# First value sums ahead of the scaled rows, products between flips and their users, and a second tensor in the row scaling: the first part of a two-layer gated cross-attention kernel

## The reference

```python
x = x + tanh(g_xattn[0]) * L0_xattn(layernorm(x), ctx)     # this part
x = x + tanh(g_ffn[0])   * L0_ffn(layernorm(x))            # shared GEGLU (this part), 8 experts by argmax
x = x + tanh(g_xattn[1]) * L1_xattn(ctx, ctx, layernorm(x))
x = x + tanh(g_ffn[1])   * L1_ffn(layernorm(x))
```

```python
Q = (x @ Wq.T).reshape(16, 16).T        # [i, h]
K, V = likewise from ctx                # [j, h]
A = softmax(einsum('ih,jh->ij', Q, K) / 4)
out = einsum('ij,jh->ih', A, V).T.reshape(256) @ Wo.T
```

## Time and profile before

| | |
|---|---|
| median of 3 runs | 764.0 us (761.69 to 764.12) |
| the profiled execution's own time | 763.81 us |
| its span in the trace | 762.0 us |
| busy in the span | PE 91%, PEld 78%, DVE 83%, POOL 55%, ACT 51% |
| the first part | 0 to about 316 us |
| mean granted TensorE clock | 0.98 |

### The profile page before, as it was taken

The page is one execution under the profiler, slowest core; times in us unless marked ns, Lnnn a source line. Parts: engine busy times, 40 slices in busy tenths (PEclk is TensorE's granted clock), DMA queues, the critical chain, the costliest instruction groups (busy, mean ns, idle before and its releaser), DMA issues.

```text
span 762.0 us, 12814 instructions
## 1 busy us (share of the span) xinstructions
PE 693.1 (91%) x4381; PEld 591.8 (78%) x4381; DVE 633.2 (83%) x927; ACT 392.3 (51%) x699; POOL 422.1 (55%) x304
## 2 busy tenths in 40 slices
PE   6749999999999989889999999999976999999996
PEld 4428878787878778657788888888865999989986
DVE  3889999999999964789999999999887777678653
ACT  2313443344343421247777777777743565555643
POOL 3788888888888881413998666667032111110000
PEclk9958999999999999989999999999999999999999
DMA  9501010011118012140544426100010101000000
GB/s 274 215 15 42 29 28 28 28 28 34 49 40 348 8 62 70 31 172 16 199 157 180 182 91 249 29 28 22 15 35 28 39 19 56 29 28 8 16 15 21
DMA packets 28642, 56.43 MB, mean 74 GB/s; under 512 B 3408, under 2 KB 24656, under 8 KB 27440
## 3 DMA queue, kind: packets, MB, share of 16 engines
q1 hardware_dynamic: 23408, 47.64, 17.6%
q0 software_dynamic: 1872, 5.11, 2.4%
q10 hardware_dynamic: 3312, 3.02, 1.2%
HBM read 48.55 MB, written 7.21 MB: 73 GB/s over the span
## 4 chain that ended last, share of the span: by engine, by line
PE 49%; DVE 19%; POOL 12%; issue 10%; ACT 7%; DMA 2%; DVEq 0%; SPq 0%; POOLq 0%; ACTq 0%
PE bank L747 19%; PE bank L738 16%; PE bank L999 9%; POOL PRODV L624 8%; PE bank L755 4%; DVE PRODQ L1562 2%; POOL PRODV L626 2%; DVE SLOT_r L1950 2%; DVE bank L1571 2%; DVE PRODV_r L1950 2%; DVE bank L1652 2%; DVE STC L2038 1%; ACT L1468 1%; ACT XS L1468 1%; ACT L1288 1%
## 5 line engine op out<-in xcount | busy, mean ns | idle before, releaser
L624 POOL TENSOR_TENSOR PRODV<-SHARED 128x2048 f32<-128x2048 f32 x32 | 144.7, 4522 | 30.4 <-DVE bank L1652 25.0
L738 PE MATMUL bank<-ROWS,SLOT 128*128 128x128 f32 x1024 | 122.9, 279 | 0.0
L738 PEld LDWEIGHTS bank<-ROWS,SLOT 128*128 128x128 f32 x1024 | 120.5, 195 | 0.8
L717 POOL TENSOR_TENSOR RS<-VE,MHALF 128x2 f32<-128x2 f32 x16 | 13.1, 819 | 149.3 <-DVE VE L2045 149.3
L626 POOL TENSOR_TENSOR PRODV<-PRODV 128x1024 f32<-128x1024 f32 x32 | 74.7, 2336 | 2.5
L1571 DVE TENSOR_REDUCE bank<-PRODQ 128x256 f32<-128x4096 f32 x16 | 70.7, 4419 | 0.1
L1562 DVE TENSOR_TENSOR PRODQ<-bank,SHARED 128x4096 f32<-128x4096 f32 x16 | 70.6, 4413 | 0.0
L1950 DVE TENSOR_TENSOR PRODQ_r<-SLOT,ROWS_r 128x1024 fp32r<-128x1024 f32 x44 | 63.5, 1472 | 0.8 <-ACT ROWS_r L1375 0.6
L641 POOL DMA_INDIRECT XS<-normal_rows,INV x23 | 26.8, 1164 | 64.5 <-PE bank L755 42.8
L738 PE MATMUL bank<-SLOT,HA 128*128 128x256 f32 x256 | 58.3, 381 | 2.4 <-DVE HA L1760 2.4
L1950 DVE TENSOR_TENSOR W_r<-SLOT,PRODQ_r 128x1024 fp32r<-128x1024 f32 x44 | 58.6, 1332 | 1.7 <-ACT PRODQ_r L1342 1.7
(11 more groups left out here) (275 smaller groups left out, 1912.1 us busy)
## 6 DMA issues: line engine op xcount, KB each, us to landing
SLOT<-wexp SPq DMA_DIRECT2D x9, 3072.0 KB, 11.6
ROWS<-xT SPq DMA_DIRECT2D x16, 128.0 KB, 2.3
SHARED<-ctxT SPq DMA_DIRECT2D x16, 128.0 KB, 2.3
X<-x SPq DMA_DIRECT2D x16, 128.0 KB, 2.6
normal_rows<-ROWS SPq DMA_DIRECT2D x16, 128.0 KB, 1.7
WET<-ctxT SPq DMA_DIRECT2D x4, 512.0 KB, 7.8
out<-X SPq DMA_DIRECT2D x16, 128.0 KB, 1.7
expert_rows<-YS ACTq DMA_DIRECT2D x12, 128.0 KB, 1.7
```

The lines of the kernel that those rows point to most:

```text
L624: gp.tensor_tensor(o, pr, v, ALU.mult).then_inc(s["av_prod"], 1)
L738: last = pe.matmul(dst, lhs(k), rhs(k), start=(k == 0), stop=(k == chunks - 1))
```

## The change

Four edits, all in the functions of the first part.

1. DVE: the value sums leave `attended` and become `value_sums(t2, hf)`. The first one now stands ahead of `normal_rows(t3)`, the second behind it, then `shares`, `add_shared`, and `attended` last.
2. DVE: smaller moves. `add_attended(t3)` goes ahead of `mult(t4, 1)`, `guarded_first(t0)` ahead of the moments, `exp_sums(t2)` ahead of `guarded(t3)`.
3. DVE: the row scaling takes the inverse root as a second tensor, spread over 256 columns, in a scalar_tensor_tensor, where it took it as a second scalar of a tensor_scalar.
4. PE: `up_half(t4, 1)` stands between the flip of AO and `out_rows(t3)`; `queries(t0)` stands between the flip of XH and `gate(t3)`, and in step 1 behind `pair_products`.

```diff
 [PE, step]
                     attended(t3)
-                    out_rows(t3)
                 if t4 is not None:
                     up_half(t4, 1)
+                if t3 is not None:
+                    out_rows(t3)
...
-                    if not first(t0, 1):
-                        queries(t0)
                     if first(t0, 2) and not first(t0, 1):
                         pair_products()
                 if t4 is not None:
                     down_rows(t4)
                 if t3 is not None:
                     normal_rows(t3)
+                if t0 is not None and not first(t0, 1):
+                    queries(t0)
                 if t3 is not None:
                     gate(t3)
                     up_half(t3, 0)
 [DVE, normal_rows]
-                dve.tensor_scalar(XH[:, t3[1], :], X[:, n3, :], MV[:, 1, 0:1], MV[:, 1, 3:4],
-                                  ALU.subtract, ALU.mult).then_inc(s["xn2_ready"], 1)
+                dve.scalar_tensor_tensor(XH[:, t3[1], :], X[:, n3, :], MV[:, 1, 0:1], spread(MV[:, 1, 3:4], 1, D),
+                                         ALU.subtract, ALU.mult).then_inc(s["xn2_ready"], 1)
 [DVE]
+            def value_sums(t2, hf):
+
+                H2 = NH // 2
+                dve.wait_ge(s["av_half"], 2 * num(t2) + hf + 1)
+                dve.tensor_reduce(
+                    AOV[:, :, hf * H2:(hf + 1) * H2],
+                    PRODV[:, :].rearrange("p (f i h j) -> p f i h j", f=2, i=DK, h=H2)
+                    [:, hf, :, :, 0:DK // 2], AX.X, ALU.add).then_inc(s["av_read"], 1)
 [DVE, step]
+                if t3 is not None:
+                    add_attended(t3)
                 if t4 is not None:
                     mult(t4, 1)
-                if t3 is not None:
-                    add_attended(t3)
...
+                if t0 is not None:
+                    guarded_first(t0)
                 if t3 is not None:
                     moments(t3, 1, "ln2")
                 if t1 is not None:
                     shift(t1)
+                if t2 is not None:
+                    exp_sums(t2)
                 if t3 is not None:
                     guarded(t3, 1, "ln2")
-                if t0 is not None:
-                    guarded_first(t0)
                 if t2 is not None:
-                    exp_sums(t2)
-                    shares(t2)
+                    value_sums(t2, 0)
                 if t3 is not None:
                     normal_rows(t3)
                 if t2 is not None:
-                    attended(t2)
+                    value_sums(t2, 1)
+                    shares(t2)
                 if t4 is not None:
                     add_shared(t4)
+                if t2 is not None:
+                    attended(t2)
```

More of the change, by code:

```diff
@@ L1643, in shares @@
                 dve.reciprocal(RI[:, :], SM[:, 1, :]).then_inc(s["recip"], 1)
+            AOV = AOP.rearrange("p (i h) -> p i h", i=DK)
+            def value_sums(t2, hf):
[5 more added lines that the diff above has]
+                    [:, hf, :, :, 0:DK // 2], AX.X, ALU.add).then_inc(s["av_read"], 1)
             def attended(t2):
                 n2 = num(t2)
[L1648 to L1655, removed]
                 dve.wait_ge(s["av_read"], 2 * n2 + 2)
@@ L1659, in attended @@
                     dve.wait_ge(s["aT_done"], n2)
-                dve.tensor_tensor(AO[:, :].rearrange("p (i h) -> p i h", i=DK), aov,
+                dve.tensor_tensor(AO[:, :].rearrange("p (i h) -> p i h", i=DK), AOV,
                                   spread(RI[:, :].rearrange("p (i o) -> p i o", o=1), 2, NH),
@@ L1722, in drain @@
                 mult(a, 1)
+                value_sums(c, 0)
+                value_sums(c, 1)
                 attended(c)
```

## The result

The changed kernel takes **785.1 us** (median of 4, 784.65 to 786.83) against 763.5 us for the kernel before: a ratio of 1.026, 95% interval 1.023 to 1.029. Forecast were 756.0 us and a range of 749.5 to 762.0, so both missed, and on the wrong side. The third rival, the scaled rows that lose a race to POOL's product, named the mechanism at a chance of 0.13 and gave it 777.5 us. It is what happened, 8 us dearer.

The account below looks back on a forecast made before the run. POOL's root, DVE's scaled rows, its first value sum and POOL's next product bound the loop in a ring, 16.68 us a step. 3.7 - 11.0 - 0.5 = -7.8 on 763.8 gave 756.0 us, range 749.5 to 762.0.

Parts of the forecast that it names:

- third rival: In the loop POOL's product starts first and DVE's scaled rows stand 4.5 us every other step: 777.5 us, chance 0.13.
- What bounds the kernel: First part's loop: POOL and DVE wait on each other, 16.68 us a step; PE, at 16.41, has 0.3 of room.
- POOL's ring: Loop: POOL's root, DVE's scaled rows, DVE's first value sum, POOL's next product, each waiting for the last; 16.68 us.
- PE's step: PE's time per loop step: 16.41 us before the change, with 0.3 us of room; forecast 15.4 after it.
- DVE's step, 15.7 us: Loop: DVE's own work, 15.76 us with small terms off and on, bounds next at 15.7, 1.0 less a step.
- It decides when DVE's step falls below 15.35 us: Loop: below this DVE step, POOL's product can start ahead of the scaled rows, which then stand still.
- POOL's product starts 0.5 us after the scaled rows: Loop: with this start of POOL's product, the next root ends at 15.4 us, 0.3 before DVE wants it.
- The price of a loss, 17.65 us a step: Loop: a loss holds DVE 4.5 us every other step, averaging 17.65 us, +0.95 a step.
- 2 x 15.4: Loop: two steps of 15.4 us, the part of the 17.65 us average without the 4.5 us of standing still.
- The first scaled rows: Ahead of the loop: first scaled rows held 4.5 us by POOL's product; tile 1's come at 75.4 us, +3.7.
- The start: Step 1: pair products no longer stand behind `queries`, so POOL's first product comes at 23.8 us, 1.6 earlier.
- The sum: +3.7 at tile 1, -11.0 for eleven steps, -0.5 to the last `mult`: -7.8 on 763.8, so 756.0 us.

Follow-up runs that it names:

- the runs with one edit of the two: Kernel before with PE's new order alone: 765.1 us; changed kernel with PE's old order and POOL's product waiting for the scaled rows: 762.9 us.
- both maxima: Changed kernel plus two superfluous DVE maxima in each step, over 256 and over 128 columns, results unused: 757.0 us, ratio 0.987.
- the rows in PSUM: Changed kernel with the second norm's rows kept in PSUM bank 5, scaled there with two scalars, and copied to X by ACT: 749.2 us.

## Why the prediction was wrong

**What bounds the kernel** held. POOL's ring and, 0.3 us behind it, PE's step were the two bounds; the runs with one edit of the two show it.

**DVE's step, 15.7 us: the step that failed.** The steps from 74.90 over 90.14 to 105.49 us are 15.24 and 15.35. I took off 0.15 for `mult` ahead of the statistics, 0.10 for the reciprocal and 0.05 for `add_shared`, and added 0.07. Start to start, the two value sums are 2.27 instead of 2.38 us, the reciprocal 0.16 instead of 0.26, `add_shared` 0.31 instead of 0.39, `add_attended` 0.40 instead of 0.48 without its 0.15 of waiting, and the sums of the exponentials 0.32 instead of 0.44. I saw two of the five places. The value sums, `add_attended` and the sums of the exponentials had the user of their result right behind them and have other work there now; why the other two are shorter isn't shown. In the prediction's own terms this decides: it put the third rival below a step of 15.35 us, and that is where the step was. The run with both maxima gives the changed kernel a step of about the forecast's 15.7, and it takes 757.0 us. That this is within 1.0 us of the forecast is in part luck: the kernel before took 768.0 beside it, so it is 11 us less and not 7.8.

**"It decides when DVE's step falls below 15.35 us": too low as well.** It rests on the sentence that POOL's product starts 0.5 us after the scaled rows. In every second step it starts 0.70 us after them, held by the exponential, and then 15.1 us pass until DVE sees the root. Steps of 15.39 and 15.52 us lose, steps from 15.7 on win. With 15.35 the third rival looked 0.35 away from a step of 15.7; by the measured point the forecast's own step stood at its edge, and a chance of 0.13 was too small for that. The calculation of the time was good for a kernel that wins its races; the one that ran loses them.

**The price of a loss, 17.65 us a step: too low.** A pair takes 37.44 us, 18.7 a step. Two steps without a loss take 31.2 (the rows in PSUM), 0.4 more than the 2 x 15.4 of the prediction, as DVE waits that long for the root in one of them. Nearly all of the rest up to 37.44 is the 4.2 us of standing still, for which 4.5 were counted, and what follows it and was not counted: waits of 0.56 for `queries` and 1.38 for the Gelu behind a PE that had been idle. On the other hand the races of the loop start only at tile 4: after the first loss DVE is the late one, and it takes three steps to catch up.

**The first scaled rows: right.** They were held 4.2 us (4.69 against 0.48), as DVE's row was, and I had counted 4.5. Tile 1's came at 74.90 us, forecast 75.4.

**The start: at the lucky end.** POOL's first product came at 25.19 us, 0.25 earlier than before, not 1.6. In this execution DVE's first scores began only at 14.76 us, 1.6 later than in the one before, and so the exponential waited for DVE's shift and not for ACT's copies:

```profile
24.60 0.51 ACT L1289 ACTIVATE SHARED<-ROWS,ROW 128x256 f32<-128x256 f32 x1 [2.36 <-DVE ROWS L1620]
```

In the profiled executions of nine other kernels with the new order this product came at 23.61 to 25.65 us. In this one late scores held it; in the two at 25.65 the scores were early (12.39 and 13.12) and ACT's second copy of the pair products came at 24.20 instead of 21.29. The forecast of 23.8 is within what the new order gives, but it was one end of a spread of 2 us, and I had put no spread on it. A faster way from the first scaled rows to tile 1's hid the difference here: counted from their last 0.48 us (58.45) it was 16.5 us instead of 18.0.

**The sum, mended:** 0.6 less at tile 1 (74.90 against 71.76 + 3.7); from there to tile 12's rows (74.90 to 270.89) 196.0 us instead of 172.4 (183.44 - 11.0), 23.6 more; and tile 12's rows are held too, so that the last `mult` that PE waits for comes 18.3 us behind them instead of 12.2, 6.1 more. 756.0 - 0.6 + 23.6 + 6.1 = 785.1, and 785.1 was measured.

**What stays open.** No run undoes the second edit, the smaller moves on DVE, alone. By the distances above they are 0.35 us of its step (0.15, 0.08 and 0.12), so without them the step would be some 15.65, close to where the races are won; that is an estimate and wasn't tried.

## What to carry to other kernels

When an edit takes away a wait that had kept two engines apart, ask what the two do to each other once they meet, and compute who comes first in each of the two alternating steps of the loop, not on average: here 0.2 us of DVE's step decided over 29 us. Where an argument rests on a margin smaller than the error of its own sum, the rival behind that margin deserves nearly an even chance. And here the exclusion was better removed (749.2 us with the operand in PSUM, 753.2 with a wait on POOL's side) than won by timing (757.0).

## What the runs showed of the hardware

- DVE's scaled rows (128x256, full operand in SBUF), 0.40 to 0.48 us in the steps without a lost race, took 4.45 to 4.73 us beside a POOL tensor_tensor of 4.5 us (L624) that had started 0.01 to 0.23 us earlier. They were held both as a scalar_tensor_tensor (4.53 to 4.73 us) and as a tensor_scalar with two scalars (4.45 to 4.61). With the operand in PSUM the first took 0.48 us beside such a product (0.07 to 0.19 us behind its start), the second 0.54 to 0.55.
- Not every DVE instruction that reads SBUF was held: the value sum, a tensor_reduce of PRODV, took 1.22 us at 90.53 us of the changed kernel, beside a product that had started at 90.40 and took 4.61, as long as the other half's at 89.01, ahead of that product.
- The other way round the loss was small: POOL's product took 4.74 to 4.79 us when it started 0.07 to 0.11 us behind the scaled rows (both maxima), and 4.52 to 4.55 when it started 0.70 to 0.71 us behind them.
- The granted clock was 0.83 in the 20 us (160 to 180) that hold most of PE's idle 4.07 us; in the kernel before, with waits of 0.47 us behind its flips, it was 1.00 in the same 20 us.
- The table load ahead of the exponential came in one half of the unrolled loop right behind ACT's copy of K and V, with DVE's shift (L1620, to 156.52) still running (1.28 us at 156.46), and in the other only once the shift was done (1.28 us at 178.85, waiting for L1620). That makes the exponential late in every second step. Why the halves differ was not tried.
